# Three hand-overs of a routed-experts and attention kernel: bias loads first, SyncE's weight loads from the next block's start, and the order of the first attention tiles

## The chip, the cores and the metric

One core of a Trainium2 chip runs one launch of the program. The metric is the device time of that launch in microseconds (us), lower is better. Inside a profiled execution all times are us from the start of its span, durations of one instruction ns where marked.

## What is computed

The reference takes x of 32 sequences of 64 tokens with 256 features, and a condition vector of 64 values for each sequence. Cut to what matters here:

```
gate  = rmsnorm(x) @ wg_W + wg_b + (cond @ gg_W + gg_b)      # 8 experts
cw    = the two largest of softmax(gate), the rest zero
y     = sum_e cw[e] * (relu(relu(x W1[e] + b1[e]) W2[e] + b2[e]) W3[e] + b3[e])
p     = y Wv.T + bv                                           # q = k = v = p, 16 heads of 16
x     = x + softmax(p p.T / 4) p @ Wo.T + bo                  # first attention
x'    = x + attention(conditioned rmsnorm(x)); x' = x' + swiglu(conditioned rmsnorm(x'))
out   = x + slot attention, 16 slot experts, and attention of the tokens to the slots, of x'
```

All matrices are float32. Most products are made of three products of rounded halves (high x high, low x high, high x low); `mm3` on lines 84 to 89 issues them.

## The kernel before

The program is cut into blocks; each has a program of its own for each engine. At a block's end semaphores are cleared and all engines meet at a barrier (line 74).

**route** (lines 99 to 407) works out the gate, gives each token two places in a list of rows sorted by expert, and starts the first weights. On DVE a long row of small steps ends in `slot2`, four calls of `places` write matrices of places in 8 parts, and TensorE multiplies each part (line 276) into the row numbers. TensorE's helper `idle(n)` (line 228) multiplies the identity by itself n times into a spare bank; it is called with 13 behind the wait for `slot_ok`, with 3 before the ninth product of line 276, and with 24 at the end of TensorE's part of the block. Nobody reads these products. SyncE waits for the first expert's number (`units_ok`), then issues the three matrices of work unit 0 (`load_matrices`, line 426) and its two biases (`load_biases`, line 434). ScalarE makes high halves of the first matrix and of the first half of the second (line 224) as they land, and DVE subtracts to make the first matrix's low half (line 407). GpSimd gathers unit 0's rows of x (line 444), 128 rows for an instruction.

**The next block** holds the routed experts (lines 479 to 811) and both attention layers with the swiglu (lines 869 to 1880) in one program per engine. There are 23 units, j = 0 to 22, of 256 rows, or of 128 for the seven in HALVES, each with one expert's matrices of 512 KB, 1 MB and 512 KB. SyncE waits until unit 1's gathered rows have landed (line 522) and then goes through the units: matrices, for j from 3 a wait for hidden layers and results, then biases. GpSimd gathers rows and scatters results. TensorE's order is: transposes of unit 0's rows (`turn(0)`, line 565), then for each j `layer(j, 0)`, `turn(j + 1)`, `out_layer(j - 1)`, `layer(j, 1)`. `turn(1)` waits for unit 1's rows. ScalarE's order within a unit is written out in lines 702 to 726: `weight_high` of unit j + 1 stands before `hidden(j, 1, 0)`, so a matrix that has not landed holds the hidden layer of the unit before. DVE begins with `x_low(0)` and the low halves of the second and third matrices (lines 771 to 774).

**The start of attention.** TensorE computes the conditioning (line 1319), runs WARM = 34 transposes of the identity that nobody reads (line 1322), and then `turn(0)`, the keys of tile 0 (`shared_keys`, line 1111), the transposed values (`shared_values`, line 1119), `scores(0)` (line 833), `turn(1)` and from there a loop of tiles. `turn(b)` needs DVE's weighted sum of the two experts' results (`combine`, line 1686, which needs ScalarE's `weighted`, line 1444) and, for b above 0, both engines' `values` copies out of the same bank. `scores(0)` needs the masked keys, three quarters from DVE (line 1742) and one from GpSimd (line 1020). The orders written out by hand are:

```
ACT: weighted(0) tokens_turned(0) shared_keys(0) values(0) weighted(1) weight_high(3) tokens_turned(1) exps(0)
DVE: combine(0) masked(0) values(0) combine(1) weight_low(3) softmax(0) ... softmax(1) masked(1)
PE:  turn(0) shared_keys(0) shared_values(0) scores(0) turn(1) scores(1) shared_keys(1) turn_weights(0)
```

Everything behind it (slot attention, slot experts, the tokens' attention to the slots) is not touched.

Of the kernel before, what the change touches and what calls it, by code (L numbers as in the profile page):

```python
# [7 lines left out]
ALU = mybir.AluOpType  # L8
# [8 lines left out]
P = 128  # L17
# [74 lines left out]
def f32(ap):  # L92
    return ap.bitcast(F32)
# [5 lines left out]
def route(nc, g, dr):  # L99
    g.moe_scope, g.moe_sems = ExitStack(), ExitStack()  # L100
    w = expert_weights(nc, g)
    with ExitStack() as ctx:
# [72 lines left out]
        @block.sync  # L175
        def _(sp):
            sp.dma_start(g.ident[:, :], dr.ident).then_inc(ident_in, 16)
            for q in range(4):
                sp.dma_start(g.x[:, 4 * q:4 * q + 4, :], dr.x_tm[:, 4 * q:4 * q + 4, :]).then_inc(x_in[q], 16)
            sp.wait_ge(const_in, 16 * 3)  # L180
            sp.wait_ge(small_in, 16 * 7)
            sp.dma_start(g.w_small[:, :, :, :], dr.w_small).then_inc(late_in, 16)
            sp.dma_start(g.wo4[:, :, :], dr.wo4).then_inc(late_in, 16)
            sp.dma_start(g.rows[:, :, :], dr.rows.to_broadcast([P, 4, D])).then_inc(late_in, 16)
            sp.dma_start(g.cols[:, :, :], dr.cols).then_inc(late_in, 16)
            sp.dma_start(g.batchmask[:, :], dr.batchmask).then_inc(late_in, 16)
            sp.wait_ge(units_ok, 1)
            e = sp.value_load(g.tile_expert[0:1, UNIT[0]:UNIT[0] + 1], min_val=0, max_val=E1 - 1)
            load_matrices(sp, dr, w, 0, e)
            load_biases(sp, dr, w, 0, e)  # L190
            sp.wait_ge(late_in, 16 * 5)

        @block.gpsimd
# [31 lines left out]

        @block.tensor
        def _(pe):
            def idle(count):
                for _ in range(count):
                    nc.tensor.matmul(pT[0][:, 0:P], g.ident[:, :], g.ident[:, :], start=True, stop=True)  # L230

            pe.wait_ge(ident_in, 16)
            for i in range(NBODY):
                if i % 2 == 0:
# [31 lines left out]
            nc.tensor.matmul(pR[:, :, :], g.tri[:, 0:P], ohb[:, :, :], start=True, stop=True)  # L266
            nc.tensor.matmul(pS[:, :, :], g.tri[:, P:2 * P], ohb[:, :, :], start=True, stop=True).then_inc(rank_ps, 1)
            pe.wait_ge(slot_ok, 1)
            idle(13)
            pe.wait_ge(row_half_ok, 2)  # L270
            for n in range(2 * TT):
                if n == 8:
                    idle(3)
                if n % 8 == 0:
                    pe.wait_ge(on_place, n // 8 + 1)
                last = nc.tensor.matmul(pI, onplace[n // TT][:, n % TT, :], row_half[n // TT][:, n % TT, :], start=n == 0, stop=n == 2 * TT - 1)
            last.then_inc(row_ps, 1)
            idle(24)

        @block.vector  # L280
        def _(dve):
            n = [0]
# [122 lines left out]
            dve.wait_ge(row_ok, 2)  # L405
            dve.wait_ge(w.hi_ok[0], 1)
            v.tensor_tensor(w.lo[0][0][:, :], w.raw[0][0][:, :], f32(w.hi[0][0][:, :]), ALU.subtract).then_inc(w.lo_ok[0], 1)


WN = (KD * M1, KM * M1, KM * D)  # L410
# [10 lines left out]
def moved(j, a):  # L421

    return 16 * sum(len(columns(i)) for i in range(j) if i % 2 == a)


def load_matrices(sp, dr, w, j, e):

    for l in (0, 1, 2) if j == 0 or j - 1 in HALVES else (0, 2, 1):
        if j >= 2:
            sp.wait_ge(w.lo_ok[l], (j - 1) * (2 if l == 1 else 1))  # L430
        sp.dma_start(w.raw[j % 2][l][:, :], dr.w[l][bass.ds(e, 1)].rearrange("o p n -> (o p) n")).then_inc(w.raw_in[j % 2][l], 16)


def load_biases(sp, dr, w, j, e):

    sp.dma_start(w.b12[j % 3][:, :], dr.b12[bass.ds(e, 1)].rearrange("o p n -> (o p) n")).then_inc(w.b_in[j % 3], 16)
    sp.dma_start(w.b3[j % 3][:, :], dr.b3[bass.ds(e, 1)].rearrange("o p n -> (o p) n").to_broadcast([P, D])).then_inc(w.b_in[j % 3], 16)
# [41 lines left out]
def routed_experts(nc, g, dr, block, sem):  # L479
    with g.moe_scope, ExitStack() as ctx:  # L480
# [38 lines left out]

        @block.sync  # L520
        def _(sp):
            sp.wait_ge(x_in[1], moved(2, 1))
            for j in range(1, NT):
                e = sp.value_load(g.tile_expert[0:1, UNIT[j]:UNIT[j] + 1], min_val=0, max_val=E1 - 1)
                load_matrices(sp, dr, w, j, e)
                if j >= 3:
                    sp.wait_ge(h_t[1], 2 * (j - 2))
                    sp.wait_ge(y_ok, j - 2)
                load_biases(sp, dr, w, j, e)

        @block.gpsimd
        def _(pool):
# [197 lines left out]
        def _(dve):  # L730
# [38 lines left out]
                v.tensor_tensor(ys[a][:, 0:n, :], pY[:, 0:n, :], bc(b3[j % 3][:, :], 1, n), ALU.add).then_inc(y_ok, 1)  # L769

            x_low(0)
            weight_low(0, 1, 0)
            weight_low(0, 1, 1)
            weight_low(0, 2)
            for j in range(NT):
# [87 lines left out]
    return vst[u * S:(u + 1) * S, :, :, u, 0:DH].rearrange("p (a b) j d -> p a b j d", b=2)[:, :, b, :, :]  # L863


WARM = 34


def attention(nc, g, dr, block, sem):
    with ExitStack() as ctx:  # L870
# [220 lines left out]
        def _(pe):  # L1091
# [232 lines left out]
            pe.wait_ge(ada_sb, 1)  # L1324
            shared_keys(0)
            shared_values(0)
            scores(0)
            turn(1)
            for i in range(NBODY - 2):
                t = 2 * i  # L1330
                scores(t + 1)
# [98 lines left out]
        def _(act):  # L1430
# [25 lines left out]
            def tokens_turned(i):  # L1456
                act.wait_ge(x_ps, i + 1)
                if i > 0:
                    act.wait_ge(k_ps, i)
                nc.scalar.activation(xT[:, :, :], two(pC), ACT.Copy).then_inc(xT_sb, 1)  # L1460
# [118 lines left out]
            weighted(0)  # L1579
            tokens_turned(0)  # L1580
            shared_keys(0)
            values(0)
            weighted(1)
            weight_high(3)
            tokens_turned(1)
            exps(0)
            for i in range(NBODY):
                t = 2 * i
# [83 lines left out]
        def _(dve):  # L1672
# [119 lines left out]
            dve.wait_ge(ada_in, 48)  # L1792
            v.tensor_tensor(g.ada[:, :, :, :], pa, bc(adab[:, :, :], 3, NB), ALU.add).then_inc(ada_sb, 1)
            combine(0)
            masked(0)
            values(0)
            combine(1)
            weight_low(3)
            softmax(0)
            for i in range(NBODY):  # L1800
# [1049 lines left out]
```

## Time and profile before

| what | us |
|---|---|
| three runs | 910.87, 917.55, 921.18 |
| their median | 917.55 |
| the profiled execution's own time | 917.55 |
| its span in the trace | 915.8 |

The span is the time from the first to the last instruction of the trace; 1.75 us of the execution lie around it. In timelines a row gives start, duration, engine, line, operation, output and inputs, count, and in brackets how long the engine sat idle before and what released it. SPq rows are SyncE's DMA issues: the transfer goes on behind them.

### The profile page before, as it was taken

To read this page: it belongs to the slowest core of one execution; us is meant where nothing else is said; L and a number is where in the kernel's file an instruction comes from. 1 tells how busy PE (TensorE), PEld (TensorE's weight loads), DVE (VectorE), ACT (ScalarE), POOL (GpSimd) and SP (SyncE) were. 2 spreads that over 40 slices of the span, in tenths; PEclk is the share of its full clock that TensorE was granted. 3 is DMA by queue.
4 is the path that set the end of the run, shared out by engine and by line. 5 is a ranking of instruction groups with operands and counts; after the bars stand their busy time and mean duration, and the time that the engine had idled before them with its cause. 6 is when DMAs were issued, how large, how long until landed. Compare 5 with 4: busy or idle time off the path is not lost. (4 is left out here: it accounts for less than half of the span.)

```text
span 915.8 us, 20512 instructions
## 1 busy us (share of the span) xinstructions
PE 817.1 (89%) x8094; PEld 702.0 (77%) x8094; DVE 581.5 (63%) x939; ACT 510.2 (56%) x941; POOL 197.0 (22%) x243
## 2 busy tenths in 40 slices
PE   5488999999999878999999988999997984997797
PEld 5378999999999746777788878999997972462554
DVE  3756777877787456888678873454434755332396
ACT  4138788888798345676668773343333442442264
POOL 0032343345343311244212222000000000000062
PEclk9589999999999978999999999999999986998799
DMA  8058686876784123342031122000005923999432
GB/s 299 1 185 303 220 295 191 301 255 217 264 302 142 53 69 82 70 89 47 19 139 39 34 70 92 2 1 1 1 1 213 416 89 150 394 423 425 164 125 71
DMA packets 70423, 143.21 MB, mean 156 GB/s; under 512 B 42504, under 2 KB 48136, under 8 KB 62904
## 3 DMA queue, kind: packets, MB, share of 16 engines
q1 hardware_dynamic: 64224, 127.25, 39.3%
q0 software_dynamic: 4496, 12.53, 4.0%
q10 hardware_dynamic: 1608, 2.12, 0.6%
q8 instruction: 65, 1.06, 0.5%
q14 instruction: 30, 0.25, 0.1%
HBM read 128.38 MB, written 13.50 MB: 155 GB/s over the span
## 5 line engine op out<-in xcount | busy, mean ns | idle before, releaser
L541 POOL DMA_INDIRECT results_of_experts<-k_w_ff,moew_place_of x39 | 52.8, 1353 | 149.8 <-DMA results_of_experts<-k_w_ff,moew_place_of 80.2
L87 PE MATMUL moe_pH<-moe_hh,moew_wh 128*128 128x256 f32 x256 | 72.6, 283 | 2.4 <-DVE moe_hl L760 2.4
L88 PE MATMUL moe_pH<-moe_hh,moew_wl 128*128 128x256 f32 x256 | 71.7, 280 | 0.0
L89 PE MATMUL moe_pH<-moe_hl,moew_wh 128*128 128x256 f32 x256 | 71.7, 280 | 0.0
L760 DVE TENSOR_TENSOR moe_hl<-k_w_ff,moe_hh 128x512 fp32r<-128x512 f32 x64 | 44.3, 692 | 30.0 <-ACT moe_hh L697 29.3
L688 ACT ACTIVATE k_w_ff<-moe_pH,moew_b 128x256 f32<-128x256 f32 x128 | 53.3, 467 | 13.6 <-PE moe_pH L89 12.9
L740 DVE TENSOR_TENSOR moew_wl<-k_x,moew_wh 128x1024 fp32r<-128x1024 f32 x47 | 55.6, 1219 | 1.0 <-ACT moew_wh L660 1.0
L740 DVE TENSOR_TENSOR moew_wl<-moew_raw,moew_wh 128x1024 fp32r<-128x1024 f32 x44 | 52.2, 1220 | 5.9 <-ACT moew_wh L660 5.9
L1715 DVE TENSOR_TENSOR k_w_ff<-attn_pS,k_w_ff 128x512 f32<-128x512 f32 x32 | 22.1, 691 | 50.5 <-PE attn_pS L89 34.6
L87 PEld LDWEIGHTS moe_pH<-moe_hh,moew_wh 128*128 128x128 f32 x256 | 48.2, 188 | 4.1 <-DVE moe_hl L760 3.8
L87 PE MATMUL moe_pY<-moew_wh,moe_hh 128*128 128x256 f32 x156 | 46.4, 298 | 5.2 <-DVE moe_hl L760 2.6
L1489 ACT ACTIVATE attn_wh<-k_w_ff 128x512 fp32r<-128x512 f32 x32 | 20.2, 632 | 51.1 <-DVE k_w_ff L1715 51.1
L444 POOL DMA_INDIRECT k_w_ff<-in_x_tm,moew_row_of x37 | 44.9, 1215 | 16.3 <-issue 10.4
L88 PEld LDWEIGHTS moe_pH<-moe_hh,moew_wl 128*128 128x128 f32 x256 | 48.2, 188 | 0.0
L89 PEld LDWEIGHTS moe_pH<-moe_hl,moew_wh 128*128 128x128 f32 x256 | 48.2, 188 | 0.0
L660 ACT ACTIVATE moew_wh<-moew_raw 128x1024 fp32r<-128x1024 f32 x44 | 44.6, 1050 | 6.3 <-DMA moew_raw<-in_w 4.7
L1756 DVE TENSOR_REDUCE attn_mx<-attn_pS 128x16 f32<-128x1024 f32 x32 | 39.1, 1223 | 13.6 <-PE attn_pS L833 12.8
L660 ACT ACTIVATE moew_wh<-k_x 128x1024 fp32r<-128x1024 f32 x46 | 46.5, 1053 | 1.7 <-PE moe_pY L89 1.7
L89 PE MATMUL moe_pY<-moew_wl,moe_hh 128*128 128x256 f32 x156 | 44.5, 285 | 0.0
L88 PE MATMUL moe_pY<-moew_wh,moe_hl 128*128 128x256 f32 x156 | 44.4, 284 | 0.0
L1984 POOL DMA_DIRECT2D queries_of_tokens<-slots_qT x8 | 4.5, 561 | 178.5 <-ACT slots_qT L2089 178.5
L697 ACT ACTIVATE moe_hh<-k_w_ff 128x512 fp32r<-128x512 f32 x64 | 40.5, 632 | 2.0
(421 smaller groups left out, 2712.3 us busy)
## 6 DMA issues: line engine op xcount, KB each, us to landing
ring<-in_w_slot SPq DMA_DIRECT2D x10, 2048.0 KB
k_x<-in_w SPq DMA_DIRECT2D x24, 512.0 KB
k_x<-in_w SPq DMA_DIRECT2D x12, 1024.0 KB
moew_raw<-in_w SPq DMA_DIRECT2D x22, 512.0 KB
moew_raw<-in_w SPq DMA_DIRECT2D x11, 1024.0 KB
ring<-in_w_slot SPq DMA_DIRECT2D x10, 1024.0 KB
k_w_ff<-in_w_slot SPq DMA_DIRECT2D x4, 2048.0 KB
attn_gat<-results_of_experts SPq DMA_DIRECT2D x16, 256.0 KB, 3.5
```

Of the source, the lines that this page charges most:

```text
L87: nc.tensor.matmul(out, ah, bh, start=start, stop=False)
L88: nc.tensor.matmul(out, al, bh, start=False, stop=False)
L89: return nc.tensor.matmul(out, ah, bl, start=False, stop=stop)
L444: nc.gpsimd.indirect_dma_start(out=xr[:, s, :], out_offset=None, in_=rows, in_offset=bass.IndirectOffsetOnAxis(ap=g.row_of[:, q:q + 1], ax ...
L541: nc.gpsimd.indirect_dma_start(out=dr.ys, out_offset=bass.IndirectOffsetOnAxis(ap=g.place_of[:, q:q + 1], axis=0), in_=ys[j % 2][:, s, :], ...
L660: nc.scalar.activation(wh[a][l][:, n], raw_w[a][l][:, n], ACT.Copy).then_inc(wh_ok[l], 1)
L688: last = nc.scalar.activation(ht[l][:, 2 * i + m, :], pH[l][i][:, m, :], ACT.Relu, bias=b12[j % 3][:, l * KM + 2 * i + m:l * KM + 2 * i + ...
L697: nc.scalar.activation(hh[l][:, 2 * i:2 * i + 2, :], ht[l][:, 2 * i:2 * i + 2, :], ACT.Copy).then_inc(hh_ok[l], 1)
L740: v.tensor_tensor(wl[a][l][:, n], raw_w[a][l][:, n], f32(wh[a][l][:, n]), ALU.subtract).then_inc(wl_ok[l], 1)
L760: v.tensor_tensor(hl[l][:, s, :], ht[l][:, s, :], f32(hh[l][:, s, :]), ALU.subtract).then_inc(hl_ok[l], 1)
L1715: v.tensor_tensor(hf[j % 2], pH[j % 2], sg[j % 2], ALU.mult).then_inc(hf_ok, 1)
L1756: v.tensor_reduce(mx[a][:, :], pS[a][:, :, :], AX_X, ALU.max).then_inc(mx_ok, 1)
```

## The change

It has four parts. In route, the biases of unit 0 are issued before its matrices; the idle products become 9 behind `slot_ok`, none between the products of line 276, and 18 at the end; and DVE makes the low half of the first half of unit 0's second matrix there, which it did in the next block before. In the experts, SyncE waits for unit 0's rows and not for unit 1's, and the biases of units 1 and 2 are issued before their matrices. WARM becomes 80. At the start of attention, TensorE does `turn(1)` before `scores(0)`, ScalarE `weighted(1)` before `values(0)` and `tokens_turned(1)` before `weight_high(3)`, DVE `combine(1)` before `masked(0)`.

```diff
@@ route, sync
             e = sp.value_load(g.tile_expert[0:1, UNIT[0]:UNIT[0] + 1], min_val=0, max_val=E1 - 1)
+            load_biases(sp, dr, w, 0, e)
             load_matrices(sp, dr, w, 0, e)
-            load_biases(sp, dr, w, 0, e)
@@ route, tensor
             pe.wait_ge(slot_ok, 1)
-            idle(13)
+            for n in range(9):
+                nc.tensor.matmul(pT[0][:, 0:P], g.ident[:, :], g.ident[:, :], start=True, stop=True)
             pe.wait_ge(row_half_ok, 2)
             for n in range(2 * TT):
-                if n == 8:
-                    idle(3)
...
             last.then_inc(row_ps, 1)
-            idle(24)
+            for n in range(18):
+                nc.tensor.matmul(pT[0][:, 0:P], g.ident[:, :], g.ident[:, :], start=True, stop=True)
@@ route, vector
             v.tensor_tensor(w.lo[0][0][:, :], w.raw[0][0][:, :], f32(w.hi[0][0][:, :]), ALU.subtract).then_inc(w.lo_ok[0], 1)
+            dve.wait_ge(w.hi_ok[1], 1)
+            v.tensor_tensor(w.lo[0][1][:, 0:1024], w.raw[0][1][:, 0:1024], f32(w.hi[0][1][:, 0:1024]), ALU.subtract).then_inc(w.lo_ok[1], 1)
@@ routed_experts, sync
-            sp.wait_ge(x_in[1], moved(2, 1))
+            sp.wait_ge(x_in[0], moved(1, 0))
             for j in range(1, NT):
                 e = sp.value_load(g.tile_expert[0:1, UNIT[j]:UNIT[j] + 1], min_val=0, max_val=E1 - 1)
+                if j < 3:
+                    load_biases(sp, dr, w, j, e)
                 load_matrices(sp, dr, w, j, e)
                 if j >= 3:
                     sp.wait_ge(h_t[1], 2 * (j - 2))
                     sp.wait_ge(y_ok, j - 2)
-                load_biases(sp, dr, w, j, e)
+                    load_biases(sp, dr, w, j, e)
@@ routed_experts, vector
             x_low(0)
-            weight_low(0, 1, 0)
             weight_low(0, 1, 1)
@@ attention
-WARM = 34
+WARM = 80
@@ attention, tensor
             shared_values(0)
+            turn(1)
             scores(0)
-            turn(1)
@@ attention, scalar
             shared_keys(0)
+            weighted(1)
             values(0)
-            weighted(1)
+            tokens_turned(1)
             weight_high(3)
-            tokens_turned(1)
@@ attention, vector
             combine(0)
+            combine(1)
             masked(0)
             values(0)
-            combine(1)
             weight_low(3)
```

## Rows read from the trace of the kernel before

**Rows 1.** The page: busy time, share of the span and instructions of each engine.

```profile
PE 817.1 (89%) x8094; PEld 702.0 (77%) x8094; DVE 581.5 (63%) x939; ACT 510.2 (56%) x941; POOL 197.0 (22%) x243
```

**Rows 2.** Waits of TensorE from 68 to 125: us in total, times, longest.

```profile
PE moe_pY L87 <- DVE moe_hl L760: 2.6, 2, 1.3
```

**Rows 3.** Timeline of TensorE at the end of route.

```profile
49.78 7.23 PE L230 MATMUL route_pT<-k_ident 128*128 128x128 f32 x48
57.97 0.30 PE L565 MATMUL moe_pX<-k_ident,k_w_ff 128*128 128x128 f32 x1 [0.95 <-PEq L74]
```

**Rows 4.** Windows: stretch, length, PE busy, granted clock, DMA share, GB/s.

```profile
53.70:60.40 6.70, 4.25 (x36) 1.00 0.10 30
60.50:63.80 3.30, 3.30 (x18) 0.50 0.21 66
...
326.70:336.90 10.20, 8.06 (x46) 0.50 0.06 22
```

**Rows 5.** Timeline of the other engines at the end of route.

```profile
47.93 0.33 SPq L436 DMA_DIRECT2D moew_b<-in_b  x1
48.45 0.67 SPq L437 DMA_DIRECT2D moew_b<-in_b  x1
...
51.95 1.23 DVE L407 TENSOR_TENSOR moew_wl<-k_x,moew_wh 128x1024 fp32r<-128x1024 f32 x1
52.50 1.06 ACT L224 ACTIVATE moew_wh<-k_x 128x1024 fp32r<-128x1024 f32 x1 [1.45 <-DMA k_x<-in_w]
```

**Rows 6.** Timeline of the experts' first units, all engines.

```profile
59.83 0.95 POOL L444 DMA_INDIRECT k_w_ff<-in_x_tm,moew_row_of  x1 [0.30 <-issue]
...
63.70 1.34 SPq L431 DMA_DIRECT2D moew_raw<-in_w  x3
...
64.53 0.60 PE L565 MATMUL moe_pX<-k_ident,k_w_ff 128*128 128x128 f32 x4
...
73.49 1.06 ACT L660 ACTIVATE moew_wh<-moew_raw 128x1024 fp32r<-128x1024 f32 x1 [3.33 <-DMA moew_raw<-in_w]
```

**Rows 7.** Waits of GpSimd, the whole span: us in total, times, longest.

```profile
POOL results_of_experts L541 <- DMA results_of_experts<-k_w_ff,moew_place_of: 80.2, 23, 5.1
```

**Rows 8.** Timeline of the start of attention, all engines.

```profile
317.92 3.93 PE L1322 MATMUL attn_pA<-k_ident 128*128 128x128 f32 x34
...
324.57 0.66 PE L1102 MATMUL attn_pC<-k_ident,attn_yt 128*128 128x128 f32 x4 [2.72 <-DVE attn_yt L1686]
...
326.00 3.08 PE L1111 MATMUL attn_pD<-attn_xT,k_w_small 128*128 128x256 f32 x8 [0.78 <-ACT attn_xT L1460]
329.12 0.84 ACT L1511 ACTIVATE attn_kT<-attn_pD,k_cols 128x256 f32<-128x256 f32 x2 [3.26 <-PE attn_pD L1111]
329.99 1.71 DVE L1742 TENSOR_SCALAR k_w_ff<-attn_kT,attn_m 128x512 f32<-128x512 f32 x3 [5.48 <-ACT attn_kT L1511]
330.18 1.99 POOL L1020 TENSOR_SCALAR k_w_ff<-attn_kT,attn_m 128x512 f32<-128x512 f32 x1 [9.46 <-ACT attn_kT L1511]
...
331.62 0.86 DVE L1751 COPY attn_vst<-attn_pC 64x256 f32<-64x256 f32 x2
332.05 0.91 ACT L1444 ACTIVATE attn_ya<-attn_gat,k_weight 128x256 f32<-128x256 f32 x2
...
332.31 1.99 PE L833 MATMUL attn_pS<-k_w_ff,attn_kT 64*64 64x256 f32 x16 [1.12 <-POOL k_w_ff L1020]
...
337.09 1.99 PE L1111 MATMUL attn_pD<-attn_xT,k_w_small 128*128 128x256 f32 x8
...
339.99 1.71 DVE L1742 TENSOR_SCALAR k_w_ff<-attn_kT,attn_m 128x512 f32<-128x512 f32 x3 [0.27 <-ACT attn_kT L1511]
...
342.42 1.09 PE L833 MATMUL attn_pS<-k_w_ff,attn_kT 64*64 64x256 f32 x16 [0.31 <-POOL k_w_ff L1020]
```

**Rows 9.** Groups of TensorE by line, 5 to 16 and 16.1 to 16.5: xcount, busy, mean ns.

```profile
L240 PE MATMUL route_pT<-k_ident,k_x 128*128 128x128 f32 x29 | 6.9, 424 | 9.3 <-DMA k_x<-in_x_tm 5.2 <-DVE route_xT L297 4.2
...
L240 PE MATMUL route_pT<-k_ident,k_x 128*128 128x128 f32 x4 | 0.7, 304 | 0.0
```

More of the change, by code:

```diff
@@ L227, in _ @@
         def _(pe):
-            def idle(count):
-                for _ in range(count):
-                    nc.tensor.matmul(pT[0][:, 0:P], g.ident[:, :], g.ident[:, :], start=True, stop=True)
             pe.wait_ge(ident_in, 16)
```

## The prediction

> **What bounds the kernel now.** I read the page's busy times first: TensorE is busy 89% of the span [rows 1], so a saving on another engine counts only where TensorE waits for it, and a delay counts wherever TensorE stands still. The change touches two places where it stands still, and I read each in the timeline of all engines, with the windows for the granted clock.
>
> At the end of route, the 24 idle products, two passes each, run from 49.78 to 57.01, later than anything else in the block, and `turn(0)` follows 0.96 us behind them [rows 3]. ScalarE is done at 53.56, DVE at 53.18, SyncE's issues at 49.12 [rows 5]. So idle products hold the barrier. In the first units, SyncE issues unit 1's matrices only at 63.70, after unit 1's rows; ScalarE then stands 3.33 us before the second matrix, until 73.49 [rows 6]. `hidden(0, 1, 0)` is queued behind it, and TensorE's `out_layer(0)` waits twice for what follows from it, 2.6 us in all [rows 2].
>
> At the start of attention a chain alternates between engines: transposes at 324.57, keys 326.00 to 329.08, ScalarE's copy to 329.96, GpSimd's mask to 332.17, scores from 332.31 [rows 8]. The warm transposes end at 321.85, 2.7 us before the chain needs TensorE, and from 326.7 to 336.9 the granted clock is 0.50, the 1.2 GHz level [rows 4, 8].
>
> **The change part by part.** The sum is made against the profiled execution: 917.55 us, of which 915.8 are span and 1.75 lie around it. That time is also the median of the three runs.
>
> *Idle products in route.* Behind `slot_ok` and between the parts of line 276, 7 fewer: TensorE waits for DVE's `places` there, so nothing is won, and if a colder clock makes the last products late, the idle passes at the end still come last. At the end, 6 products or 12 passes fewer. They are the last ones, at full clock [rows 4]; the price of a pass I take from the 34 transposes of the same shape, (3.93 - 0.27) / 33 = 0.11 us [rows 8], so 1.3 us. TensorE would be done at 55.7.
>
> *Biases first, and the added subtraction.* The two bias issues take from 47.93 to 49.12, 1.2 us [rows 5]; in front, they shift the matrices by that much. ScalarE's copy of the second matrix's half moves from 52.50 to 53.7 and ends at 54.8, and behind it DVE now subtracts for 1.23 us, the duration of line 407 [rows 5], to 56.05. That is past TensorE's 55.7, so DVE becomes the last into the barrier: of 1.3 us, 0.95 remain. Were the shift nothing, 1.3 remain; were it 2, nearly nothing. The 1.23 us taken out of DVE's start in the next block are worth nothing: TensorE there waits for `x_low`, which stands ahead of them.
>
> *SyncE's wait.* Unit 0's rows have landed at the block's start, so the issue of unit 1's matrices follows some 1 us behind it, as from row landing to issue now, then biases for 1 us: about 59.0 in place of 63.70, 4.7 us earlier. ScalarE would need the second matrix at 70.15 less the 0.95, about 69.2 (73.49 less its 3.33 of waiting); it landed at 73.4, so now at 68.8. The stall of 3.33 goes and with it TensorE's 2.6 us. If the landing moves by less than 4.2 us, part stays: bounds 0 and 2.6, taken 2.6.
>
> What is then late? Unit 1's own rows. GpSimd's second gather ends at 60.78 [rows 6], now 59.8, and `turn(1)` comes at 64.53 now, 63.6 then [rows 6]. A gather that shares the DMA engines with matrices isn't shown for this tile; the nearest row is the scatter of line 541, whose wait for the one before is 80.2 / 23 = 3.5 us in the mean and 5.1 at the longest [rows 7]. Landing would be at 63.3 or 64.9: cost 0 to 1.3, taken 0.5. The page "DMA: Bandwidth & Descriptors" of the Trainium skill, "Queues, rings and completion order", says that each DMA engine takes turns between queues by packets; that would put the gather's packets between the matrices' and not behind them all, and is in favour of the low end.
>
> *WARM 80.* 46 more transposes by 0.11 us: the chain's `turn(0)` can start at 326.8, not 324.57: +2.2. In return the keys (8 products, 3.08 us partly at the low clock) find it high and take 1.99, as tile 1's do [rows 8]: -1.1. The keys' copy ends at 331.1, 1.1 later than now.
>
> *The order of the first tiles.* DVE has `combine(1)` ahead of `masked(0)`, and it waits for ScalarE's `weighted(1)`, 0.91 us behind the keys' copy: 332.0; with its last half 332.5. Then the mask, 1.71, to 334.2, and `values(0)`, 0.86, to 335.1 [rows 8]. GpSimd's quarter, which was last until now, is done at 333.3. On TensorE `turn(1)` waits for `values(0)`, and `scores(0)` is queued behind it. `turn(1)` runs 335.1 to 335.8, scores 1.09 us at full clock, so until 336.9; at the low clock, which I take because TensorE has stood idle since 331.9, three times as long as at this place today, until 338.2. It was 334.30. Part is paid back, since `turn(1)` is already done and `scores(1)` follows at once: DVE's two softmax pairs, 4.9 us, run without the pause they have now, and `masked(1)` starts at 341.8 or 343.2 against 339.99. The next scores, held by GpSimd's mask, start at 343.6 or 345.1 against 342.42 [rows 8]: +1.2 to +2.7. Were the clock high both before and after, the keys' 1.1 and about 0.9 of scores would not be in the time of before, and the loss would be 3.2 to 3.7. I take +2.7, the end by today's clock [rows 4]. With TensorE busy 89% of the whole span [rows 1], little behind it could take up a shift, and I let it stay to the end.
>
> Sum: -0.95 - 2.6 + 0.5 + 2.7 = -0.35, so 917.2 us. Two savings at the experts are eaten by the start of attention.
>
> **Rivals.** *The clock comes out well* (faster). TensorE runs the first layer of unit 0 at 0.50 from 60.5 to 63.8 [rows 4]. If it stays high there, 3.3 us at half rate become 1.65; if the 80 warm transposes also carry scores(0), the loss is 1.2: -0.95 - 2.6 + 0.5 - 1.65 + 1.2 = -3.5, so 914.1. For it: a shorter time without work behind the warm transposes. Against: TensorE still has two gaps at each place, and the shorter tail of idle products leaves it no busier.
>
> *The early matrices crowd out unit 1's rows* (slower). At `turn(1)` TensorE waits for a landing at 64.9, 1.3 us, and the matrices themselves, which share the engines with gathers of units 2 and 3, land no earlier than needed, so the 2.6 us stay: -0.95 + 1.3 + 2.7 = +3.05, so 920.6. It decides from a row landing past 63.6 and a second matrix past 69.2. For it: the old wait kept just these apart, and the second matrix took long even so. Against: the mean of rows 7.
>
> *Transposes don't hold the clock* (slower still). The page "TensorE: Matmul & The Clock Gate" of the Trainium skill, "Part 4: PE-mode transpose", says that transposes don't count as work for the clock. As a mechanism here: the clock falls within the 80, and 46 at the low rate (0.21 apiece, half speed) take 4.7 us more, and the keys 1.1 more: 923.0. The trace is against that rule: the transposes of line 240, nothing else on TensorE, take 424 ns each until 16, and then a mean of 304 [rows 9]; the clock rose on transposes alone. And the 34 warm ones kept their 0.11 us apiece to the last [rows 8].
>
> *The loads do not start early at all*, because SyncE stands before something else: its loop for unit 1 has no other wait, so I give it no chance apart.
>
> **How the numbers follow.** Likeliest, 0.45; good clock, 0.23; crowding, 0.2; transposes, 0.04; 0.08 for what I don't see. Runs of the kernel before lie between -0.7% and +0.4% of their median, so about 1% is what a measurement can tell from no change, 9.2 us here, and no case reaches it by itself. Faster by over 1%: 0.06; slower: 0.08; within: 0.86. The range holds all cases down to 914.1 and up to 920.6 with the runs' scatter beyond, half of it on each side: 910 to 924.
>
> **What would show each step.** Right: `turn(0)` of the experts about 57.0, with DVE's second subtraction ending last before it; unit 1's matrices issued near 59; no wait of ScalarE over 1 us for a raw matrix before 80; no 1.3 us waits of `out_layer(0)`. In attention, `turn(0)` directly behind the warm transposes, DVE's mask of tile 0 starting 1.4 us behind the keys' copy, and scores(0) behind `turn(1)`. Wrong: a wait of `turn(1)` for DMA; the keys of tile 0 at 3 us; a time outside 910 to 924, which would mean a stage behind the first tiles that reacts, or clock changes that I have not priced.

## The result: a small loss where none was expected

| | median us | lowest | highest | runs |
|---|---|---|---|---|
| kernel before | 915.66 | 910.04 | 921.18 | 20 |
| changed kernel | 921.08 | 918.6 | 926.5 | 20 |

The ratio is 1.006 with a 95% interval of 1.004 to 1.0081, which is 5.5 us more (3.7 to 7.4). That is less than the 1% which the prediction called no change and inside its range, but it is a loss and not the 0.35 us of gain that the sum gave. The figure lies near the 920.6 of the rival that had the early matrices crowd out unit 1's rows. The profiled execution took 921.89 us, its span 920.1.

The page of the changed kernel, busy time of each engine. Beside [rows 1]: TensorE has 20 records more (46 transposes, less 26 idle passes) and is busy 2.4 us longer; the other engines hardly differ, so the rest of the 4.3 us between the two spans is waiting.

```profile
PE 819.5 (89%) x8114; PEld 708.1 (77%) x8114; DVE 581.4 (63%) x939; ACT 510.7 (56%) x941; POOL 196.7 (21%) x243
```

**The end of route.** The changed kernel's timeline of all engines, from the bias loads to `turn(0)` and SyncE's next issues.

```profile
46.43 0.36 SPq L434 DMA_DIRECT2D moew_b<-in_b  x1
46.97 0.33 SPq L435 DMA_DIRECT2D moew_b<-in_b  x1
47.48 1.32 SPq L429 DMA_DIRECT2D k_x<-in_w  x3
47.76 3.60 PE L271 MATMUL route_pC<-moew_wl 128*128 128x40 f32 x16
51.20 5.83 PE L274 MATMUL route_pT<-k_ident 128*128 128x128 f32 x36
51.47 0.20 DVE L392 TENSOR_SCALAR route_upper<-route_pC 128x40 f32<-128x40 f32 x1 [1.25 <-PE route_pC L271]
...
53.00 1.06 ACT L224 ACTIVATE moew_wh<-k_x 128x1024 fp32r<-128x1024 f32 x1 [23.02 <-DMA k_x<-in_w]
54.19 1.22 DVE L403 TENSOR_TENSOR moew_wl<-k_x,moew_wh 128x1024 fp32r<-128x1024 f32 x1 [1.05 <-ACT moew_wh L224]
55.47 1.06 ACT L224 ACTIVATE moew_wh<-k_x 128x1024 fp32r<-128x1024 f32 x1 [1.41 <-DMA k_x<-in_w]
56.56 1.23 DVE L405 TENSOR_TENSOR moew_wl<-k_x,moew_wh 128x1024 fp32r<-128x1024 f32 x1 [1.15 <-ACT moew_wh L224]
58.77 0.63 PE L565 MATMUL moe_pX<-k_ident,k_w_ff 128*128 128x128 f32 x4 [1.75 <-PEq L74]
...
60.53 1.43 SPq L429 DMA_DIRECT2D moew_raw<-in_w  x3
60.63 0.95 POOL L442 DMA_INDIRECT k_w_ff<-in_x_tm,moew_row_of  x1 [0.30 <-issue]
```

Two things are late here. The last 16 placement products take 3.60 us, so TensorE is done at 57.03 although it has 12 idle passes fewer, where it was done at 57.01 [rows 3]. And the second matrix's half reaches ScalarE at 55.47, not at 52.50 [rows 5], so DVE is last, at 57.79. The barrier releases `turn(0)` at 58.77, 0.98 us behind DVE, instead of at 57.97 [rows 3]: +0.8 where the sum had -0.95. The same products in the kernel before, its timeline of TensorE:

```profile
46.60 1.07 PE L276 MATMUL route_pC<-moew_wh 128*128 128x40 f32 x8
47.73 2.21 PE L276 MATMUL route_pC<-moew_wl 128*128 128x40 f32 x16
```

**The first units.** The changed kernel's waits of TensorE, from 68 to 125 (us in total, times, longest), and the wait itself in the timeline.

```profile
PE moe_pX L565 <- DMA k_w_ff<-in_x_tm,moew_row_of: 2.8, 1, 2.8
```

```profile
68.32 1.12 PE L565 MATMUL moe_pX<-k_ident,k_w_ff 128*128 128x128 f32 x4 [2.83 <-DMA k_w_ff<-in_x_tm,moew_row_of]
69.97 2.95 ACT L660 ACTIVATE moew_wh<-moew_raw 128x1024 fp32r<-128x1024 f32 x3
```

The 2.6 us of waits behind `moe_hl` are gone, as is ScalarE's stall. In their place stands one wait of 2.8 us for unit 1's rows. Their gather left GpSimd at 61.58 and TensorE could use the rows at 68.32, 6.7 us later. Before, the same gather left at 60.78 and SyncE, which waited for its landing, issued at 63.70 [rows 6], so it took 2.9 us at most.

Behind the wait the granted clock is 0.50, from 68.3 to 71.3, where in the kernel before it is 1.00 from 65 to 72. So what goes and what comes cancel: unit 7's first transposes stand at 134.07 against 133.29, +0.8, which is what `turn(0)` had at the block's start. Up to the first `combine` of attention the shift grows to 2.5 us (326.12 against 323.63); 1.2 of it is one more wait for gathered rows, at 230.68, in code that the change doesn't touch.

**The start of attention.** The changed kernel's timeline of TensorE, then windows of it (stretch, length, busy time of PE, PEld, DVE, ACT, POOL, granted clock, DMA share, GB/s).

```profile
321.54 11.86 PE L1321 MATMUL attn_pA<-k_ident 128*128 128x128 f32 x80
333.24 0.60 PE L1101 MATMUL attn_pC<-k_ident,attn_yt 128*128 128x128 f32 x4
...
334.62 1.97 PE L1110 MATMUL attn_pD<-attn_xT,k_w_small 128*128 128x256 f32 x8 [0.78 <-ACT attn_xT L1459]
...
341.20 1.09 PE L1101 MATMUL attn_pC<-k_ident,attn_yt 128*128 128x128 f32 x4 [2.97 <-DVE attn_vst L1750]
```

```profile
316.50:327.50 11.00, 11.00 (x52) 10.71 (x51) 3.69 (x8) 1.11 (x3) 3.97 (x8) 0.50 0.33 109
327.60:341.10 13.50, 8.83 (x69) 7.86 (x67) 3.12 (x7) 3.01 (x7) 1.57 (x1) 1.00 0.12 39
```

The 80 transposes begin at 321.54 at the low clock, so they take 11.86 us and not the 9 us that 0.11 us apiece would make, and `turn(0)` stands at 333.24 against 324.57 [rows 8], +8.7. The keys then take 1.97 instead of 3.08, and `turn(1)` waits 2.97 us for DVE's values copy, which now stands behind `combine(1)` and the mask. A fixed event further on, SyncE's load of `k_w_small`, is issued at 549.45 where it was at 543.85, +5.6, as a timeline of SyncE shows in each kernel. Of the 8.7 us, 3.1 are gone by there. The third scores stand at 350.95 against 342.42 [rows 8], +8.5, or +6.0 without the 2.5 us that the experts bring; the prediction had +2.7.

### The profile page after: what moved, and what is told of

It is laid out like the page before. It is cut to its first block and busy times, and to the rows that moved or that the text cites. A ratio compares the mean times of both kernels' runs of the same rounds, so it can differ in the third digit from the quotient of the medians.

```text
span 920.1 us, 20552 instructions
## 1 busy us (share of the span) xinstructions
PE 819.5 (89%) x8114; PEld 708.1 (77%) x8114; DVE 581.4 (63%) x939; ACT 510.7 (56%) x941; POOL 196.7 (21%) x243
## 5 line engine op out<-in xcount | busy, mean ns | idle before, releaser
L541 POOL DMA_INDIRECT results_of_experts<-k_w_ff,moew_place_of x39 | 55.6, 1425 | 146.2 <-DVE k_w_ff L769 83.2
L442 POOL DMA_INDIRECT k_w_ff<-in_x_tm,moew_row_of x37 | 42.9, 1161 | 20.7 <-issue 9.1
```

Of the source, the lines that this page charges most:

```text
L442: nc.gpsimd.indirect_dma_start(out=xr[:, s, :], out_offset=None, in_=rows, in_offset=bass.IndirectOffsetOnAxis(ap=g.row_of[:, q:q + 1], ax ...
L541: nc.gpsimd.indirect_dma_start(out=dr.ys, out_offset=bass.IndirectOffsetOnAxis(ap=g.place_of[:, q:q + 1], axis=0), in_=ys[j % 2][:, s, :], ...
```

## The experiments

Each ratio is to the kernel before, measured beside it on the same chip. Edits are to the kernel before unless said otherwise.

### The four parts alone

SyncE's wait and the biases of units 1 and 2:

```diff
-            sp.wait_ge(x_in[1], moved(2, 1))
+            sp.wait_ge(x_in[0], moved(1, 0))
...
+                if j < 3:
+                    load_biases(sp, dr, w, j, e)
```

> Only SyncE's part: it waits for unit 0's rows, and biases of units 1 and 2 go first. Theory crowding: unit 1's rows land late among unit 1's matrices, TensorE waits 2 to 4 us at turn(1) of the experts for DMA, and since the 2.6 us of waits at out_layer(0) go, the time is within 1 us of the kernel before. Rival (the late rows are the doing of route's later end, not of the loads): no wait at turn(1), and 2 to 3 us less than before.

Ratio 0.998 (0.9963 to 0.9997). The waits of TensorE, from 57.9 to 125:

```profile
PE moe_pX L567 <- DMA k_w_ff<-in_x_tm,moew_row_of: 3.1, 1, 3.1
...
```

With nothing else changed the matrices crowd out the rows: 3.1 us of waiting for them, and none for `moe_hl`. The price of the crowding was not 0.5, and it eats the 2.6 us: from `turn(0)` to unit 7's first transposes it is 75.63 us (58.34 to 133.97) against 75.32 before. The ratio says 0.2% less time, but this trace doesn't show a gain where the edit is; what it is ahead by lies behind the experts, in code that this run leaves as it was.

The warm transposes, `WARM = 34` to `WARM = 80`:

> Only WARM = 80. Theory: the 80 transposes end 5 us later at full clock and up to 8.7 us later where the clock is low at their start; the chain of tile 0 starts 2.5 to 6 us later and gets 2 to 4 back from a high clock in keys and scores, so +1 to +3 us. Rival (the clock it buys pays for all): 0 or less.

Ratio 1.0008 (0.9987 to 1.0029). Its windows, before and behind the rise of the clock, and a later one:

```profile
313.40:323.50 10.10, 10.10 (x48) 9.81 (x48) 2.81 (x6) 1.02 (x4) 3.96 (x8) 0.50 0.28 87
323.60:337.00 13.40, 10.02 (x85) 9.04 (x87) 3.53 (x8) 3.52 (x9) 1.99 (x1) 1.00 0.18 61
340.00:380.00 40.00, 35.09 (x436) 26.64 (x430) 33.22 (x52) 25.29 (x46) 9.73 (x6) 0.99 0.35 73
```

The same later window of the kernel before:

```profile
340.00:380.00 40.00, 35.14 (x426) 26.19 (x427) 30.56 (x49) 23.82 (x44) 10.22 (x6) 0.91 0.35 74
```

Here too the transposes take 11.05 us and put `turn(0)` at 330.04, 5.5 us late, yet the time hardly moves. Keys and scores at full clock give back some of it; and in the 40 us behind, the clock is 0.99, not 0.91, which at TensorE's 35 us of work is another 3 or so. In this one trace that is enough for the rest. It is not the warm transposes that bring the 0.99: sync_only, which leaves attention as it was, has 1.00 there.

```profile
340.00:380.00 40.00, 35.49 (x456) 27.13 (x454) 33.49 (x55) 26.09 (x48) 9.92 (x7) 1.00 0.41 83
```

Of the runs below that leave attention as it was, route_no_bias, idle_last and rows_early have 1.00 there too, split_loads and half_rows_early 0.91. The spell of low clock comes and goes with 34 warm transposes.

The order of the first tiles on all three engines, as in the change:

> Only the order of the first tiles on TensorE, ScalarE and DVE. Theory: DVE's mask of tile 0 starts 1.4 us behind the keys' copy in place of at once, and scores(0) start 3 us later behind turn(1); some of it is paid back, +1 to +3 us. Rival (turn(1) early lets the second tile's chain run ahead): 0 or less.

Ratio 1.0032 (1.0011 to 1.0052), +2.9 us. `turn(0)` stood at 325.45, the keys took 1.97, `turn(1)` came at 333.46 after a wait of 2.97 for DVE's values copy, scores of both tiles ran from 334.02 to 337.43, and the third scores started at 342.80 against 342.42 [rows 8]. That this is late shows better beside sync_only, whose keys also took 1.97: from DVE's first `combine` to the third scores it is 18.28 us (324.52 to 342.80) against 16.37 (324.08 to 340.45), 1.9 more.

The route part, that is biases first, idle products 9, 0 and 18, and the added subtraction:

> Only route's part: biases first, 27 idle products for 40, the added subtraction. Theory late landing: the first matrix lands 1.2 to 3 us later, DVE's second subtraction ends at 56 to 57.8 and holds the barrier, so turn(0) comes at 57.0 to 58.8 against 57.97: -1 to +1 us. Rival (idle products alone hold the barrier): turn(0) at 56.6, -1.3 us.

Ratio 1.0022 (0.9998 to 1.0047). ScalarE's second copy starts at 54.90 and DVE's second subtraction at 55.99, so DVE is done at 57.22, TensorE at 57.35, and `turn(0)` stands at 58.73, 0.8 us later than before, as in the changed kernel. But it stands 1.38 us behind TensorE, not 0.95, so neither of the two was the last. What is left is GpSimd's second gather, which left the engine at 55.69; rows_early below has the same more strongly.

### What in route costs the time

The same without the bias move:

> Route's part without its first edit: matrices before biases as before, 27 idle products, the added subtraction. Theory (the two small loads in front are what makes the block end late): ScalarE's second copy at 52.5, DVE's subtraction done by 55, turn(0) at 56.6 to 57.2 against 58.73 with the biases first: 1 to 2 us less than the whole of route's part. Rival (fewer idle products leave the clock low, and that is what costs): turn(0) near 58 or later all the same.

Ratio 1.0028 (1.0002 to 1.0054). The timeline of TensorE and a window of it:

```profile
47.90 3.58 PE L274 MATMUL route_pC<-moew_wl 128*128 128x40 f32 x16
51.31 6.72 PE L230 MATMUL route_pT<-k_ident 128*128 128x128 f32 x36
58.99 0.63 PE L565 MATMUL moe_pX<-k_ident,k_w_ff 128*128 128x128 f32 x4 [0.95 <-PEq L74]
```

```profile
46.50:51.50 5.00, 5.00 (x25) 0.50 0.91 344
```

The matrices land in time now (ScalarE at 52.00 for the second), DVE is done at 55.7, and TensorE itself is last: its 36 idle passes take 6.72 us instead of 5.4 (36 of 48 times the 7.23 of [rows 3]), since the clock is still 0.50 when they begin. `turn(0)` is no earlier. Which idle products are missed? First the front ones alone taken out:

```diff
-            idle(13)
+            idle(9)
...
-                if n == 8:
-                    idle(3)
```

> The kernel before with the idle products behind slot_ok cut from 13 to 9 and the 3 between the products of line 276 gone; the last 24 stay. Theory clock: the clock is at 0.50 while the placement products run, the last of them end 1.3 us or more later than at full clock, row numbers and TensorE's last idle products come later, turn(0) at 58.5 or later against 57.97, +1 to +2 us. Rival (these products fill time in which TensorE waits anyway): turn(0) where it was, within 0.5 us.

Ratio 1.0041 (1.0021 to 1.0061). Timeline of TensorE:

```profile
43.95 3.67 PE L274 MATMUL route_pC<-moew_wh 128*128 128x40 f32 x16 [1.01 <-DVE moew_wh L376]
47.45 3.58 PE L274 MATMUL route_pC<-moew_wl 128*128 128x40 f32 x16
50.86 7.38 PE L230 MATMUL route_pT<-k_ident 128*128 128x128 f32 x48
59.19 0.63 PE L563 MATMUL moe_pX<-k_ident,k_w_ff 128*128 128x128 f32 x4 [0.95 <-PEq L74]
```

Windows of it, where the front products are missing and behind it:

```profile
39.70:44.00 4.30, 3.29 (x17) 3.02 (x15) 4.27 (x5) 0.00 (x0) 0.00 (x0) 0.50 0.00 0
46.00:51.00 5.00, 5.00 (x25) 5.00 (x25) 3.18 (x10) 1.06 (x1) 0.00 (x0) 0.50 0.90 338
```

Before, TensorE is busy the whole 4.30 us of the first of these stretches, the clock is at 0.57 in it and, in that trace, at 1.00 in the products. TensorE had time for the idle products, and without them the last 16 products go from 2.21 to 3.58 us, the row numbers are over a microsecond late, and `turn(0)` 1.2. Then the last ones alone, `idle(24)` to `idle(18)`:

> The kernel before with only the last idle products cut from 24 to 18. Theory: they hold the barrier, turn(0) 1.3 us earlier, and the time 1 us less. Rival (the tail is what brings the clock back up): turn(0) earlier but unit 0's first layer at the low clock for longer, within 0.5 us or slower.

Ratio 1.0021 (0.9996 to 1.0047). `turn(0)` stands at 57.49, only 0.5 us earlier. But this trace came to the products at a lower clock, with all the front idle products in place; so did sync_only, whose route is the kernel's before. Rows of idle_last, then of sync_only:

```profile
47.06 2.85 PE L276 MATMUL route_pC<-moew_wl 128*128 128x40 f32 x16
49.74 6.79 PE L230 MATMUL route_pT<-k_ident 128*128 128x128 f32 x36
```

```profile
46.56 3.03 PE L276 MATMUL route_pC<-moew_wl 128*128 128x40 f32 x16
49.42 7.96 PE L230 MATMUL route_pT<-k_ident 128*128 128x128 f32 x48
```

A fairer measure is the time from the first idle product behind `slot_ok` to `turn(0)`. It is 18.4 us in four traces whose route is untouched (before, warm80_only, order_pe_kept, split_loads) and 19.9 in two (sync_only, order_only), 18.65 in idle_last and 20.5 in idle_front. Beside the two traces with the same colder products idle_last gains 1.25 us, which is the 1.3 of the prediction. It is then lost: two waits for `moe_hl`, of 2.9 and 1.3 us, stand in the first units, where the kernel before has 1.3 twice, and no gain is seen in the time. idle_front is 0.6 to 2.1 us late by this measure.

### What in the order costs the time

ACT and DVE in the new order, TensorE in the old:

> The kernel before with the new order on ScalarE and DVE only; TensorE keeps scores(0) before turn(1). Theory (both halves cost: combine(1) in front delays the mask by 1.3 us, and scores(0) behind turn(1) adds values(0) and the transposes, 1.5 to 2 us): about half of the loss of the whole order change, +1 us. Rival (the loss is all in the mask behind combine(1)): as much as the whole order change, +2 to +3 us.

Ratio 1.0052 (1.0029 to 1.0075). Its timeline around the mask:

```profile
328.89 1.09 DVE L1686 SCALAR_TENSOR_TENSOR attn_yt<-attn_gat,k_weight,attn_ya 128x256 f32<-128x256 f32 x2 [5.85 <-ACT attn_ya L1444]
329.90 1.36 DVE L1742 TENSOR_SCALAR k_w_ff<-attn_kT,attn_m 128x512 f32<-128x512 f32 x3
331.36 1.98 PE L833 MATMUL attn_pS<-k_w_ff,attn_kT 64*64 64x256 f32 x16 [2.19 <-DVE k_w_ff L1742]
333.27 1.11 PE L1102 MATMUL attn_pC<-k_ident,attn_yt 128*128 128x128 f32 x4
```

With `turn(0)` at 324.18, the mask starts at 329.90, behind `combine(1)`, and scores wait 2.19 us for it. The loss is at least as large as with all three engines changed, so it lies in the new order of DVE and ScalarE, which waits for `combine(1)` ahead of the mask, and not in `turn(1)` ahead of `scores(0)` on TensorE, which rather gives some back (the two intervals overlap). What DVE's and ScalarE's halves cost apart was not measured.

### Rows against matrices

All of unit 1's rows gathered in route, behind unit 0's, so that SyncE's early wait holds for both:

```diff
@@ route, gpsimd
+            gather_rows(nc, g, dr, w, xr[:, 1, :, :], 1)
@@ routed_experts, sync
-            sp.wait_ge(x_in[1], moved(2, 1))
+            sp.wait_ge(x_in[0], moved(1, 0))
@@ routed_experts, gpsimd
-            gather_rows(nc, g, dr, w, xr[1], 1)
```

> The kernel before, with unit 1's rows gathered in route, behind unit 0's, and SyncE waiting for unit 0's rows only. Theory crowding: with the rows out of the way of the matrices there is no wait for DMA at turn(1) and none of the 1.3 us waits at out_layer(0), so 2 to 3 us less than before. Rival (the early matrices gain nothing, something else holds ScalarE): the waits at out_layer(0) stay or move, within 1 us of before.

Ratio 0.9973 (0.9948 to 0.9999). Timeline of TensorE:

```profile
49.50 7.23 PE L231 MATMUL route_pT<-k_ident 128*128 128x128 f32 x48
59.65 0.63 PE L565 MATMUL moe_pX<-k_ident,k_w_ff 128*128 128x128 f32 x4 [2.92 <-PEq L74]
```

Neither rows nor `out_layer(0)` are waited for in the first units, but the barrier at route's end is: it comes 1.7 us late, although TensorE is done at 56.73 and GpSimd's last issue at 56.24. Nothing but the gathers' landing is left for it to wait for. Taking 0.95 us off `turn(0)`, the barrier was free 2.5 us behind the last gather's issue here, and 2.1 us behind it in route_only and in half_rows_early below. Splitting the matrices instead (unit 1's first at the block's start, the other two behind unit 1's rows) avoids that:

> The kernel before, where SyncE issues unit 1's first matrix (512 KB) at the block's start and the other two only behind unit 1's rows. Theory crowding by bytes in the queue: the rows land at most 1.2 us later, no or little wait at turn(1), and ScalarE's wait for the second matrix shrinks by 1 to 1.5 us, so -1 us. Rival (any matrix in front holds the rows): TensorE waits over 1 us at turn(1) and nothing is won.

Ratio 0.9973 (0.9947 to 1.0), so no gain is quite shown. No wait for rows at `turn(1)`, one of 1.2 us left for `moe_hl`. And the middle way, the first 128 of unit 1's rows in route and the other 128 in the next block, with SyncE's early wait:

```diff
@@ route, gpsimd
+            gather_rows(nc, g, dr, w, xr[:, 1, :, :], 1, (0,))
@@ routed_experts, sync
-            sp.wait_ge(x_in[1], moved(2, 1))
+            sp.wait_ge(x_in[0], moved(1, 0))
@@ routed_experts, gpsimd
-            gather_rows(nc, g, dr, w, xr[1], 1)
+            gather_rows(nc, g, dr, w, xr[1], 1, (1,))
```

> As rows_early, but only the first 128 of unit 1's rows are gathered in route, the second 128 in the next block as before; SyncE waits for unit 0's rows only. Theory: the block's end waits for what was gathered in it, so with one gather fewer turn(0) comes at 58.0 to 58.5 against 59.65 in rows_early, the second half lands before turn(1), and the time is 3 to 4 us less than before. Rival (the second half is crowded as both were): 2 us or more of wait for DMA at turn(1), no gain on rows_early.

Ratio 0.996 (0.9933 to 0.9986), 910.98 us (907.38 to 914.99 in 12 runs) beside 914.77: better than both kernels. Its timeline of TensorE:

```profile
58.17 0.63 PE L568 MATMUL moe_pX<-k_ident,k_w_ff 128*128 128x128 f32 x4 [1.29 <-PEq L74]
...
65.87 0.66 PE L568 MATMUL moe_pX<-k_ident,k_w_ff 128*128 128x128 f32 x4 [0.97 <-DMA k_w_ff<-in_x_tm,moew_row_of]
```

The barrier costs 0.3 us (1.29 against 0.95), the rows 0.97, and the 2.6 us are gone. From `turn(0)` to unit 7's first transposes it is 72.20 us (58.17 to 130.37) against 75.32 before, 3.1 less, so here the gain does show where the edit is.

The changed kernel with SyncE's old wait put back tests crowding from the other side:

> The changed kernel with only SyncE's old wait back (for unit 1's rows). Theory crowding with nothing net: the 2.8 us wait at turn(1) goes and the waits at out_layer(0) of 2.6 us come back, within 1 us of the changed kernel. Rival (the early loads are the cause of the changed kernel's loss): 2 us less or more than the changed kernel.

Ratio 1.0085 (1.0052 to 1.0117). No wait for rows at `turn(1)`, but the other waits are back: 1.3 us at `moe_pY` for `moe_hl`, and before it 1.9 for a low half of a matrix and 1.4 for `moe_hl`. With the old wait the changed kernel is no faster, so the early loads are not what makes its loss.

### The changed kernel with parts undone

The idle products at 13, 3 and 24 again:

> The changed kernel with the 13, 3 and 24 idle products back. Theory (fewer idle products in front leave the clock low while the placement products run, and that is the larger part of the loss at route's end): placement products end by 50.1, row numbers 1.2 us earlier than in the changed kernel, turn(0) at 57.9 to 58.4 because late matrices then hold DVE, ratio to the kernel before about 1.003 for the changed kernel's 1.006. Rival (biases first costs as much by itself): ratio stays at 1.005 or more.

Ratio 1.0084 (1.0055 to 1.0113). Timelines of TensorE and of DVE:

```profile
48.23 2.20 PE L274 MATMUL route_pC<-moew_wl 128*128 128x40 f32 x16
50.27 7.23 PE L277 MATMUL route_pT<-k_ident 128*128 128x128 f32 x48
59.22 0.63 PE L568 MATMUL moe_pX<-k_ident,k_w_ff 128*128 128x128 f32 x4 [1.71 <-PEq L74]
```

```profile
57.02 1.22 DVE L408 TENSOR_TENSOR moew_wl<-k_x,moew_wh 128x1024 fp32r<-128x1024 f32 x1 [1.15 <-ACT moew_wh L224]
```

The products are back at 2.20 us, and nothing is won: the late matrices alone hold DVE until 58.24 and `turn(0)` until 59.22. This execution comes to the products 0.5 us later than the kernel before (48.23 against 47.73); less that, `turn(0)` stands at 58.7, just where the changed kernel has it. The order on all three engines put back:

> The changed kernel with the old order of the first attention tiles on all three engines. Theory (combine(1) in front of the mask costs 3 us): ratio to the kernel before about 1.003. Rival (behind 80 warm transposes the order is hidden, and WARM is what costs): ratio stays at 1.005 or more.

Ratio 1.006 (1.0032 to 1.0088): `turn(0)` of attention at 330.12 and the first scores at 336.69, where WARM 80 alone has 330.04 and 336.61. With the old order back the time is no better than the changed kernel's, which speaks against the order as its cause; the next run speaks for it. Both put back:

> The changed kernel with both back; what is left of the change is biases first, the moved subtraction, SyncE's early loads and WARM 80. Theory (these two are the whole loss): ratio 0.997 to 1.001. Rival (a third cause): 1.002 or more.

Ratio 1.0028 (1.0005 to 1.0052). What is left in it, late matrices, WARM 80 and the wait for rows, costs 2.6 us (0.5 to 4.7). It was measured beside after_idles_back, and the order is all that differs between the two: 922.14 (6 runs) against 917.02 (12 runs), 5.1 us in the medians.

## Why the prediction was wrong, step by step

Three steps failed: route's, where -0.95 came out at +0.8 (a colder clock in the placement products, and matrices 3.0 us late behind the biases instead of 1.2); the gather beside early matrices, priced at 0.5, whose 2.8 us of waiting ate the 2.6 saved; and WARM 80, whose transposes were all priced at full clock.

No one part of the change makes the 5.5 us. The four parts alone give -0.20, +0.08, +0.32 and +0.22%, together +0.42%, and their intervals add up (as the root of their squares) to 0.42 either way, so the measured 0.60% needs no interaction of parts. (They share one measure of the kernel before, so the true interval is a little wider, some 0.45.) How much each has within the changed kernel is not settled to better than some 2 us: the idle products and the order give back about 0.3 points when both are undone, and one at a time nothing beside the changed kernel.

The traces, cut at three marks, say where the profiled execution lost its 4.3 us against the one before. The marks are `turn(0)`, the start of DVE's first `combine`, and SyncE's issue of `k_w_small`.

| stretch | before | changed | difference | the sum had |
|---|---|---|---|---|
| start to `turn(0)` | 57.97 | 58.77 | +0.8 | -0.95 |
| to the first `combine` | 265.66 | 267.35 | +1.7 | -2.6 + 0.5 |
| to `k_w_small` | 220.22 | 223.33 | +3.1 | +2.7 |
| to the end | 371.9 | 370.7 | -1.2 | 0 |

So the first two terms had the wrong sign, and the third looks right, but by luck.

Nine traces in all leave the start of attention as it was, and their third stretch takes 214.3 to 220.2 us, 216.8 in the mean; the kernel before has the longest. With WARM 80 alone changed there it takes 216.4 to 224.2 in three traces (mean 220.4), with the new order alone 218.2 in one, with both 220.1 to 223.9 in three (mean 222.5). By the means the start of attention costs 5.7 us, most of the loss, and not 3.1; the scatter of 6 us in untouched code makes that an estimate, good to some 3 us.

- **Idle products in route.** This step failed. It said that fewer of them behind `slot_ok` and between the products win and lose nothing, and that if a colder clock made the last products late, the idle passes at the end would still come last. They do come last or nearly so, but later by what the products lose. The clock was colder (0.50 where it was 1.00), the 16 products took 3.60 instead of 2.21 us, and the idle passes that follow ran partly at half rate too. In all six traces without the front idle products these 16 take 3.58 or 3.60; with them 2.20 or 2.21 in eight traces and 2.85 to 3.03 in three. So the 1.3 us saved at the end (1.25 in idle_last) were spent by the front ones (0.6 to 2.1 in idle_front). The idle products fit into TensorE's waiting, as the prediction said, but they also keep a clock, which it put at nothing. It also left GpSimd out of what the barrier waits for: the second gather's issue ended at 54.03 before, and by the 2.1 to 2.5 us of the runs above its landing alone would hold the barrier until 56.1 to 56.5, where the sum had 56.05.
- **Biases first.** Right that DVE becomes last in the changed kernel, wrong in size: a shift of 1.2 us was taken, and "were it 2, nearly nothing" would be left. The three issues moved by 1.1 us, from 46.4 to 47.48, but the first matrix landed 3.0 us later, 53.00 against 49.99, and the second 55.47 against 52.50. Windows of the two kernels over the same 3.5 us, the changed one first:

```profile
46.40:49.90 3.50, 3.21 (x18) 3.11 (x19) 3.40 (x10) 0.00 (x0) 0.00 (x0) 0.68 0.19 45
```

```profile
46.40:49.90 3.50, 3.37 (x28) 3.00 (x27) 3.40 (x10) 0.00 (x0) 0.00 (x0) 1.00 0.70 257
```

  While the bias loads are under way the core moves 45 GB/s, not 257. They are 4 KB and 128 KB, and the larger took 4.1 us from issue to landing; that the big transfers start behind the small ones is read from this and not tested. The term was -0.95 and came out at +0.8. Each of the two steps alone holds the barrier (58.99 without the bias move, 59.22 with the idle products back), which may be why undoing one shows nothing.
- **SyncE's wait.** The stall and both waits are gone, as said, and where the rows are out of the way -2.6 is about right: 3.1 us less up to unit 7 in half_rows_early, with 0.97 of waiting left. In the changed kernel it came out at nothing, by the next step.
- **The gather beside matrices.** The step that carried 0.5, bounds 0 and 1.3, failed: 2.3 to 4.7 us in the five kernels with early matrices and the gather beside them, and a low clock behind it. The nearest row, scatters at a mean of 3.5 us, was none of a gather that starts as 2 MB of matrices do. The page "DMA: Bandwidth & Descriptors" of the Trainium skill, "Queues, rings and completion order", has the engines take turns between queues by packets, which the prediction read in favour of the low end; the 6.7 us from the end of the gather's issue to its use speak against that reading. With it the crowding rival was right that the rows come late, with 2.8 us for its 1.3, and wrong that the 2.6 us stay. The runs give it no loss in time: together with the waits that go it is -0.2%. That its 920.6 was near the measured time was luck.
- **WARM 80 and the order.** The +2.7 stood for both together. Alone the order measures +2.9 (1.0 to 4.8) and WARM 80 +0.7 (-1.2 to 2.7). The order's mechanism is the one of the step, DVE's `combine(1)` ahead of the mask, and that `turn(1)` waits on DVE's copy was foreseen at 3.2 us (335.1 less 331.9) and measured at 2.97. WARM 80's step failed: it had all 46 more transposes at 0.11 us and `turn(0)` at 326.8. It came at 333.24, since the transposes began at the low clock: 80 of them take 8.95 to 11.86 us in six traces. The spells of clock behind that repaid part come in kernels with 34 warm transposes too.
- **Transposes and the clock.** The rival by which transposes don't count as work for the clock, with the page "TensorE: Matmul & The Clock Gate" of the Trainium skill, "Part 4: PE-mode transpose", fell. From 321.54 TensorE does nothing but transposes; the granted clock is 0.50 until 327.5 and 1.00 from 327.6. It rose on them.
- **No change of over 1%.** Right, and the range held, but with the sign wrong: -0.35 forecast, +5.5 (3.7 to 7.4) measured. The 921.08 lies only 3.9 us above the forecast of 917.2, since the sum began at the one profiled execution of 917.55 and the median of twenty runs before is 915.66; the change itself was missed by 5.8. In the traces the sum erred by 1.75 us in route and by 3.8 between `turn(0)` and the first `combine`, 2.1 of them by unit 7.

Late in the changed kernel's trace, 843 to 878 has the clock at 0.90 where the same untouched work (835 to 870 before) had 0.76, and of a shift that was 7.2 us at 800, 4.3 are left at the end. Nothing in the change reaches there, so single traces differ by 3 us for no cause in the change. Only ratios over many runs carry the verdicts above; what the traces say of sizes is as rough as their scatter.

## What to carry to other kernels

Price filler products by the clock of what runs behind them, not by the time that they occupy: 7 idle products that lay wholly beside another engine's work were worth 0.6 to 2.1 us at the next barrier. Small loads ahead of big ones delay these by more than their issue time, so put them in front only if nobody waits for the big ones. When a bulk load is freed to start earlier, look for the small indirect transfer that starts beside it and move that ahead, in a size that the block's end doesn't have to wait for. And before a difference of two traces is put down to an edit, look at the same stretch in traces where it is untouched: here nine of them spread over 6 us, as much as the whole loss.

## What the runs showed of the hardware that was not expected

- A gather of 256 rows took 2.9 us at most from the end of its issue to its landing before the matrices, and 6.7 us to its use beside them.
- Two bias loads, 4 KB and 128 KB, whose issues shift the matrices' by 1.08 us, delayed the landing of the matrices behind them by 3.0 us.
- The placement products ran back to back and the clock stayed at 0.50 (the windows of route_no_bias and idle_front, with TensorE busy all of 5 us); with the idle products ahead and between, the last 16 took 2.20 or 2.21 us in eight of eleven traces, at 1.00 in the kernel before, and 2.85 to 3.03 in three.
- The barrier at a block's end waits for gathers issued in that block: 2.92 us of idle TensorE in rows_early against 0.95 [rows 3], with all engines done. The barrier is free 2.1 to 2.5 us behind the last gather's issue in rows_early, half_rows_early and route_only. This is found by exclusion, no row names it.
